# Turning the next block's input on VectorE instead of TensorE in an mLSTM + MLP kernel

## What is computed

```python
xn = layernorm(x)                       # per token, no scale or shift
q, k, v = xn @ Wq.T, xn @ Wk.T, xn @ Wv.T
i_pre, f_pre = soft_cap(xn @ Wig.T + big), soft_cap(xn @ Wfg.T + bfg)
h = mlstm_scan(q, k, v, i_pre, f_pre)   # 8 heads, a state that is carried from token to token
attn = (sigmoid(xn @ Wog.T) * multihead_norm(h, gamma)) @ Wout.T
ffn = (silu(xn @ w_gate.T) * (xn @ w_up.T)) @ w_down.T      # 2048 hidden features
return x + attn + ffn
```

## Time and profile before

| | |
|---|---|
| median of three runs | 3138.32 us |
| the profiled execution | 3138.3 us |
| its span, first to last instruction | 3136.5 us |
| TensorE busy | 3084.2 us, 98% |
| VectorE, ScalarE, GpSimd busy | 61%, 36%, 24% |
| before the first block's gates | 73.6 us |
| first block | 100.1 us |
| each of the 30 blocks between | 95.4 us |
| last block with the tail | 100.6 us |

### The profile page before, as it was taken

One profiled execution on the slowest core, in us unless ns is written; L12 is line 12 of the kernel. 1 busy time (PEld: TensorE's weight loads), 2 busy tenths in 40 slices (PEclk: granted clock), 3 DMA queues, 4 the chain that ended last, 5 costly groups with the idle time before them and its releaser, 6 DMA issues.

```text
span 3136.5 us, 61859 instructions
## 1 busy us (share of the span) xinstructions
PE 3084.2 (98%) x22474; PEld 2240.3 (71%) x22474; DVE 1907.1 (61%) x4377; ACT 1126.0 (36%) x2160; POOL 751.1 (24%) x1120
## 2 busy tenths in 40 slices
PE   4999999999999999999999999999999999999999
PEld 2677777777777777777777777777777777777776
DVE  8666656656556656555666566565566665565665
ACT  6333333333333333333333333333233333333332
POOL 4222222222222222222222222212222212222222
PEclk9999999999999999999999999999999999999999
DMA  5000000000000000000000000000000000000000
GB/s 222 8 14 13 13 7 7 13 13 13 13 6 8 13 13 13 7 7 13 13 13 13 7 7 13 13 13 13 0 13 13 13 13 7 7 13 13 13 13 7
DMA packets 20334, 51.09 MB, mean 16 GB/s; under 512 B 1506, under 2 KB 1634, under 8 KB 18274
## 3 DMA queue, kind: packets, MB, share of 16 engines
q1 hardware_dynamic: 20322, 50.95, 4.4%
HBM read 34.16 MB, written 16.78 MB: 16 GB/s over the span
## 4 chain that ended last, share of the span: by engine, by line
PE 97%; DVE 1%; ACT 1%; issue 0%; DMA 0%; SPq 0%; DVEq 0%; ACTq 0%
PE work L1082 21%; PE work L1084 21%; PE work L1083 21%; PE acc L1083 7%; PE acc L1084 7%; PE acc L1082 7%; PE o_bank L1195 3%; PE o_bank L1255 2%; PE work L1261 2%; PE s_bank L1242 1%; PE work L1273 1%; PE work L1267 1%; PE e_bank L1236 1%; PE work L1172 1%; PE work L1227 1%; DVE amax L740 1%
## 5 line engine op out<-in xcount | busy, mean ns | idle before, releaser
L1082 PE MATMUL work<-xt,weights 128*128 128x256 f16 x4608 | 1256.0, 273 | 0.5 <-DVE arena L958 0.5
L1084 PE MATMUL work<-xt,weights 128*128 128x256 f16 x4608 | 1256.0, 273 | 0.0
L1083 PE MATMUL work<-xt,weights 128*128 128x256 f16 x4608 | 1255.9, 273 | 0.0
L543 POOL TENSOR_TENSOR arena<-arena 128x256 f16<-128x256 f32 x512 | 348.4, 680 | 1715.7 <-ACT arena L678 1715.7
L955 DVE SCALAR_TENSOR_TENSOR arena<-arena,work 128x256 f32<-128x256 f32 x512 | 215.2, 420 | 538.1 <-ACT arena L674 534.9
L1082 PEld LDWEIGHTS work<-xt,weights 128*128 128x128 f16 x4608 | 478.5, 104 | 69.9 <-DVE arena L958 0.7
L1083 PEld LDWEIGHTS work<-xt,weights 128*128 128x128 f16 x4608 | 450.9, 98 | 69.5
L1084 PEld LDWEIGHTS work<-xt,weights 128*128 128x128 f16 x4608 | 450.8, 98 | 52.2
L674 ACT ACTIVATE arena<-work,unscale 128x256 f32<-128x256 f32 x512 | 241.7, 472 | 585.6 <-PE work L1084 585.2
L678 ACT ACTIVATE arena<-arena 128x256 f16<-128x256 f32 x512 | 213.3, 417 | 592.2 <-DVE arena L958 592.2
L1082 PE MATMUL acc<-weights,arena 128*128 128x512 f16 x1024 | 388.1, 379 | 0.4 <-POOL arena L543 0.4
(11 more groups left out here) (214 smaller groups left out, 4038.1 us busy)
## 6 DMA issues: line engine op xcount, KB each, us to landing
arena<-x_dram SPq DMA_DIRECT2D x33, 512.0 KB, 3.3
out_dram<-arena SPq DMA_DIRECT2D x32, 512.0 KB, 2.8
weights<-w_g_dram SPq DMA_DIRECT2D x4, 1024.0 KB, 12.6
weights<-w_u_dram SPq DMA_DIRECT2D x4, 1024.0 KB, 20.4
arena<-w_d_dram SPq DMA_DIRECT2D x4, 1024.0 KB, 26.8
arena<-w_qk_dram SPq DMA_DIRECT2D x1, 1024.0 KB, 5.8
arena<-w_v_dram SPq DMA_DIRECT2D x1, 1024.0 KB, 7.8
weights<-w_o_dram SPq DMA_DIRECT2D x1, 1024.0 KB, 25.3
```

Source lines behind the costliest of these rows:

```text
L543: g.tensor_tensor(hh[:, j % HB, 1, :], tt[:, j % 2, :], hh[:, j % HB, 0, :], ALU.subtract).then_inc(h_ready, 1)
L1082: t.matmul(dst, w[0], a[0], start=first, stop=False, skip_group_check=True)
L1083: t.matmul(dst, w[0], a[1], start=False, stop=False, skip_group_check=True)
L1084: return t.matmul(dst, w[1], a[0], start=False, stop=last, skip_group_check=True)
```

## The change

The next input's two chunks are no longer transposed by TensorE. VectorE turns each in sixteen pieces: one instruction takes 32 tokens and one 32-feature slice of each of the four 128-feature groups, turns the four 32x32 squares, and writes them to another group of 32 partitions (`turn`). Four calls of `turn` make a chunk. Three stand behind tile 5 and one behind tile 6 for chunk 0, three behind tile 7 and one behind tile 9 for chunk 1. For that the statistics' `mean_var` goes from tile 5 to tile 3, `xn0` from tile 6 to 4 and `xn1` from tile 9 to 6. `xn` and its turned form lie in SBUF space of the block that is free by then, so the high and low parts (`xT0`, `xT1` on ScalarE and VectorE, still behind tile 15) read SBUF and not PSUM. They wait for `hoT1` on TensorE, after which nothing in the block reads `xt`.

`USES` loses `xT0` and `xT1`; `att1` gets bank 1 by name. The gates wait for both low parts through `xt_ready`. On VectorE alone, behind tile 10, `pv2` comes before `es3`.

```diff
 USES = ([... "ffn12", "st3", "o1",
-         "ffn13", "att0", "ffn14", "ffn15", "hoT1", "xT0", "xT1", "att1"])
+         "ffn13", "att0", "ffn14", "ffn15", "hoT1", "att1"])
+BANK = {name: n % 3 for n, name in enumerate(USES)}
+BANK["att1"] = 1

-AFTER[3] = ["wT", "stack3"]
-AFTER[4] = ["wbc", "kT", "es0"]
-AFTER[5] = ["o0", "mean_var"]
-AFTER[6] = ["es1", "pv0", "xn0"]
+AFTER[3] = ["wT", "stack3", "mean_var"]
+AFTER[4] = ["wbc", "kT", "es0", "xn0"]
+AFTER[5] = ["o0", "turn00", "turn01", "turn02"]
+AFTER[6] = ["es1", "pv0", "turn03", "xn1"]
+AFTER[7] = ["turn10", "turn11", "turn12"]
 AFTER[8] = ["es2", "pv1", "center0"]
-AFTER[9] = ["scale0", "xn1"]
+AFTER[9] = ["scale0", "turn13"]
 AFTER[10] = ["heads0", "es3", "pv2"]
+DVE_AFTER[10] = ["heads0", "pv2", "es3"]

+            def turn(dst, src, q):
+                tokens = slice(q * 32, (q + 1) * 32)
+                for r in range(P // 32):
+                    features = src[tokens, :].rearrange("t (k r f) -> t r k f", k=KC, f=32)[:, r, :, :]
+                    d.transpose(dst.rearrange("p (k t) -> p k t", k=KC)[r * 32:(r + 1) * 32, :, tokens],
+                                features).then_inc(xn_turned, 1)

 (ScalarE)
                         elif step.startswith("xT"):
-                            wait_full(act, i, step)
-                            x_high(i + 1, k, bank(step)[:, :])
+                            wait_full(act, i, "hoT1")
+                            act.wait_ge(xn_turned, START + (i * NCH + k + 1) * TURNS)
+                            x_high(i + 1, k, xnt[k])

 (TensorE)
-                pe.wait_ge(work_free[bank_no("xT1")], START + i * uses_of(bank_no("xT1")))
+                pe.wait_ge(xt_ready, NCH * (i + 1))
...
-                        elif step.startswith("xT"):
-                            pe.wait_ge(xn_ready, NCH * (i + 1) + k + 1)
-                            for n in range(KC):
-                                tr = t.transpose(bank(step)[:, n * P:(n + 1) * P], xn[:, k, n * P:(n + 1) * P],
-                                                 ident[:, :])
-                            tr.then_inc(work_full, 1)
```

More of the change, by code:

```diff
@@ L56 @@
          "ffn6", "st0", "ffn7", "ffn8", "st1", "ffn9", "ffn10", "st2", "ffn11", "hoT0", "ffn12", "st3", "o1",
-         "ffn13", "att0", "ffn14", "ffn15", "hoT1", "xT0", "xT1", "att1"])
+         "ffn13", "att0", "ffn14", "ffn15", "hoT1", "att1"])
 NUSE = len(USES)
-assert NUSE % 3 == 0
+BANK = {name: n % 3 for n, name in enumerate(USES)}
+BANK["att1"] = 1
 def bank_no(name):
-    return USES.index(name) % 3
+    return BANK[name]
 def uses_of(b, before=NUSE):
-    return len(USES[b:before:3])
+    return len([name for name in USES[:before] if BANK[name] == b])
 AFTER = {j: [] for j in range(NJ)}
@@ L95 @@
 AFTER[15] = ["hoT1", "xT0", "xT1"]
+TURNS = 16
+DVE_AFTER = {j: list(steps) for j, steps in AFTER.items()}
+DVE_AFTER[10] = ["heads0", "pv2", "es3"]
 UNIT_IN = {j + 1: int(step[-1]) for j in AFTER for step in AFTER[j] if step.startswith("pv")}
@@ L229, in mlstm_mlp_kernel @@
                  ("hof", 512), ("hoh", 512), ("kp", 512), ("tt", 512), ("hh", 768), ("res", 1024),
-                 ("wtok", NCH * 72), ("xn", NCH * D), ("qq", 1024), ("kk", 1024),
+                 ("wtok", NCH * 72), ("qq", 1024), ("kk", 1024),
                  ("state", NG * GW), ("wr", 256), ("tg", 256), ("uhl", 256), ("xin", 1024)]
@@ L239, in mlstm_mlp_kernel @@
             at[name] = arena[:, starts[name]:starts[name] + n]
-        assert 5 * SLOT + GCOLS <= starts["xn"]
+        assert 5 * SLOT + GCOLS <= starts["qq"]
         def in_arena(n):
@@ L256, in mlstm_mlp_kernel @@
         xin = at["xin"].rearrange("p (c d) -> p c d", c=NCH)
-        xn = at["xn"].rearrange("p (c d) -> p c d", c=NCH)
+        xn_first = at["kk"].rearrange("p (c d) -> p c d", c=NCH)
+        xn = at["qs"], at["kf"]
+        xnt = at["kp"], arena[:, starts["lf"]:starts["lf"] + D]
         qs = at["qs"].rearrange("p (g t) -> p g t", g=NG)
@@ L331, in mlstm_mlp_kernel @@
         xt_hi = sem("xt_hi")
+        xn_turned = sem("xn_turned")
         xt_ready = sem("xt_ready")
@@ L514, in _ @@
             link(g.memset(uhl, 0.0))
+            pool.wait_ge(first_xt, NCH)
             for name in ("qq", "kk", "wr", "tg", "state"):
@@ L519, in _ @@
             for n, started in enumerate((*work_free, out_stored, res_done, exp_done, p_ready, num_ready, ho_ready,
-                                         state_ready)):
+                                         state_ready, xn_turned)):
                 g.memset(begun[0:1, n:n + 1], 0.0).then_inc(started, START)
@@ L604, in x_high, with norm_x @@
                              ACT.Copy).then_inc(xt_hi, 1)
-            def norm_x(i, c):
-                act.wait_ge(factors_ready, i + 1)
-                s.activation(xn[:, c, :], xin[:, c, :], ACT.Identity, bias=shift[:, c:c + 1],
+            def norm_x(dst, c):
+                s.activation(dst, xin[:, c, :], ACT.Identity, bias=shift[:, c:c + 1],
                              scale=rstd[:, c:c + 1]).then_inc(xn_ready, 1)
+            act.wait_ge(factors_ready, 1)
             for c in range(NCH):
-                norm_x(0, c)
+                norm_x(xn_first[:, c, :], c)
                 act.wait_ge(first_xt, c + 1)
@@ L710, in _ @@
                         elif step.startswith("xn"):
-                            norm_x(i + 1, k)
+                            if k == 0:
+                                act.wait_ge(factors_ready, i + 2)
+                                act.wait_ge(qi_ready, i + 1)
+                            else:
+                                wait_full(act, i, "kT")
+                            norm_x(xn[k], k)
                         elif step.startswith("xT"):
-                            wait_full(act, i, step)
-                            x_high(i + 1, k, bank(step)[:, :])
+                            wait_full(act, i, "hoT1")
+                            act.wait_ge(xn_turned, START + (i * NCH + k + 1) * TURNS)
+                            x_high(i + 1, k, xnt[k])
                 own.close()
@@ L800, in means, with x_low @@
                     d.bn_aggr(mean_var[:, c, :], bn6[:, c, :]).then_inc(stats_ready, 1)
-            def x_low(i, c, src, done):
+            def turn(dst, src, q):
[4 more added lines that the diff above has]
+                                features).then_inc(xn_turned, 1)
+            def x_low(i, c, src):
                 dve.wait_ge(xt_hi, NCH * i + c + 1)
                 d.tensor_tensor(xt[:, :, 1, c * P:(c + 1) * P], src.rearrange("p (k t) -> p k t", k=KC),
-                                xt[:, :, 0, c * P:(c + 1) * P], ALU.subtract).then_inc(done, 1)
+                                xt[:, :, 0, c * P:(c + 1) * P], ALU.subtract).then_inc(xt_ready, 1)
             back = 1.0 / (XS * WS)
@@ L825, in _ @@
             for c in range(NCH):
-                x_low(0, c, (e_bank, s_bank)[c][:, :], xt_ready)
+                x_low(0, c, (e_bank, s_bank)[c][:, :])
             scales(0)
@@ L960, in _ @@
                                            op1=ALU.mult).then_inc(free_of(f"ffn{j}"), 1)
-                    for step in AFTER[j]:
+                    for step in DVE_AFTER[j]:
                         k_ = int(step[-1]) if step[-1].isdigit() else 0
@@ L1061, in _ @@
                         elif step.startswith("xT"):
-                            wait_full(dve, i, step)
-                            x_low(i + 1, k_, bank(step)[:, :], free_of(step))
+                            x_low(i + 1, k_, xnt[k_])
+                        elif step.startswith("turn"):
+                            c = int(step[-2])
+                            dve.wait_ge(xn_ready, NCH * (i + 1) + c + 1)
+                            turn(xnt[c], xn[c], k_)
                         elif step == "att0":
@@ L1105, in _ @@
                 for k in range(KC):
-                    tr = t.transpose((e_bank, s_bank)[c][:, k * P:(k + 1) * P], xn[:, c, k * P:(k + 1) * P],
+                    tr = t.transpose((e_bank, s_bank)[c][:, k * P:(k + 1) * P], xn_first[:, c, k * P:(k + 1) * P],
                                      ident[:, :])
@@ L1141, in _ @@
             pe.wait_ge(w_split_act, len(PE_LOW))
-            pe.wait_ge(xt_ready, NCH)
             with pe.Fori(0, NB) as i:
```

## The result

| | time, us | block in the loop, us |
|---|---|---|
| kernel before | 3139.22, median of 4 runs (3137.84 to 3140.45) | 95.41 |
| changed kernel | 3115.12, median of 4 runs (3114.46 to 3116.27) | 94.68 |
| forecast | 3114.6 (3109 to 3128) | 94.67 |

The ratio is 0.9924 with a 95% interval from 0.9913 to 0.9936: 0.76% faster. The profiled execution has a span of 3112.7 us against 3136.5, 23.8 us less.

What follows compares the result with a forecast made beforehand. TensorE, busy 98% of the span, was taken to bound the kernel. 3138.3 - 28.2 (transposes) + 4.3 (bank of `att1`) + 0.2 (`mean_var`) = 3114.6 us, range 3109 to 3128 us; the turns cost nothing.

Steps and rivals of the forecast that it cites:

- The sum: Whole kernel: 3138.3 - 28.2 + 4.3 + 0.2 = 3114.6 us, 0.76% less.
- The transposes: TensorE before `down(14)`: eight float32 transposes gone, 0.88 us in each of 32 blocks, 28.2 us less.
- The bank of `att1`: Behind the gates: `q` waits for VectorE's drain of `att1`, 0.14 us, 31 times, 4.3 us.
- The turns' price: VectorE: 32 turns a block at 0.31 us each, 9.9 us a block; bounds 0.21 and 0.45 us a turn.
- Where they lie: VectorE, tiles 5 to 10: tile 7's L955 0.24 us late, tile 8's 0.9, last four turns end at 1570.9.
- `heads0`: VectorE behind tile 10: ends 1.3 us later, at 1574.5 and not 1573.18, still in time for `hoT0`.
- The spare time: `heads0` ends about 1.0 us before TensorE wants its result for `hoT0` at 1575.52.
- the first rival: Turns too slow: spare time gone at 0.36 us a turn, slower than before from 0.40; 3172 us at 0.45; chance 0.09.
- The exchange: VectorE behind tile 10, `pv2` before `es3`: L997 in front would take some 0.7 us of tile 12's spare 1.0.
- `mean_var`: Moved behind tile 3, it delays tile 4's L955 and L958 by 0.24 us; costs 0.24 us once, first block.
- `down(15)`: Comes 0.88 us earlier against GpSimd's low part: just fits; if not, some 0.1 us a block, 3 us in all.

Runs made afterwards that it cites:

- experiment 1: Changed kernel with `att1` in bank 2 in place of bank 1: 3110.76 us, ratio 0.9911 to the kernel before.
- experiment 6: Changed kernel with the turned squares written back to the 32 partitions they come from (output not the reference's): 3115.44 us.
- Experiment 4: Changed kernel with four more turns behind tile 7, into a buffer nothing reads: 3117.85 us; with eight more: 3159.61 us, ratio 1.0067.
- experiment 3: Changed kernel with eight transposes put back on TensorE behind `hoT1`, read by nobody: 3143.69 us, ratio 1.0016 to the kernel before.
- experiment 5: Changed kernel with `es3` before `pv2` on VectorE again: 3116.70 us; with four more turns behind tile 7 as well: 3159.76 us.

## Why the prediction was right, point by point

- **The sum.** Forecast 23.7 us less. The 32 blocks are 23.2 us shorter: 0.69 in the first, 0.73 in each of the 30 between, 0.71 in the last. The stretch ahead of the first block's gates is 0.6 us shorter (73.02 against 73.63) and makes it 23.8. The edit has no part in that: in the eight edits of the changed kernel this stretch takes from 73.4 to 75.6 us. That the total met the forecast within 0.5 us is in part luck; that the block did within 0.01 is not.
- **The transposes.** Forecast 28.2 us; put back, they cost 28.6. Right.
- **The bank of `att1`.** Forecast 0.14 us a block and 4.3 us; the trace shows 0.14 and experiment 1 gives back 4.4. Right, in place and size, and the 0.06 us from a release in the first block holds at q (1593.61 to 1593.67).
- **The turns' price.** I took 0.31 us from copies over 32 partitions and it is 0.33: 10.6 us a block and not 9.9. The form of the term (duration and hold) is what the trace shows. VectorE's busy time went up by 273.7 us and not 287: the turns are 309.4, but `heads0` has become shorter (below). The estimate of 0.34 from the Trainium skill ("VectorE: DVE Perf Modes", "The three transpose paths", with the hold) was the nearer one. The Trainium skill's rule on the same page, "Two Vector instructions with no wait between them", that an output in another quadrant (group of 32 partitions) than the last one's holds the instruction, agrees with experiment 6. The Trainium skill's advice there to give 128x128 transposes to TensorE ("Rules for kernel authors") does not hold here: 10.6 us on VectorE are free where 0.88 us on TensorE are not.
- **Where they lie.** Tile 7's L955 was to be 0.24 us late and is 0.35 (1544.23 + 11.33 against 1555.21); tile 8's 0.9 and is 1.2 (1549.02 + 11.33 against 1559.12); the last four turns were to end at 1570.9 and end at 1571.3. This follows from 0.33 in place of 0.31.
- **`heads0`.** Here a term was mis-sized, to the safe side. It was to end 1.3 us later than before and ends 0.9 later (1562.77 + 11.33 = 1574.10 against 1573.18), although the turns before it were slower. I moved its three instructions with the durations that they had. L1046 and the one behind it stood beside GpSimd's low part and mask and took 0.62 and 1.22 us; now L1070 is done before the low part begins (1561.42), L1073 overlaps it for its last 0.28 us, and they take 0.16 and 0.69. The last one takes 0.95 and not 0.69. Together 0.73 us less, against 0.34 us by which `heads0` begins later than forecast. That GpSimd's neighbourhood makes the difference is read from these coincidences; no run tests it. That the two errors of the prediction have opposite signs is luck.
- **The spare time.** Forecast 1.0 us, measured 1.42 to the end of the record. I charged no release there. Experiment 4 shows 0.15 us for it, which leaves 1.27. The threshold of 0.36 us a turn from the first rival is by this 0.33 + 1.27 / 20 = 0.39, worked out and not tried in this form.
- **The exchange.** The prediction had `es3` in front take 0.7 us of the spare time at tile 12. Without the exchange the drain of `st2` ends 1.5 us nearer to tile 12, as the scores also wait 0.75 us for GpSimd's mask, a wait that the prediction left out. All of the 1.51 us are used up, and the exchange is just needed.
- **`mean_var`.** Forecast 0.24 us once. In the first block q has no wait yet, and with the transposes put back (experiment 3) it is 0.20 us longer than before. In the changed kernel it is 99.43 us against 100.12, 0.69 less: 0.88 less 0.20 is 0.68. Right.
- **`down(15)`.** Forecast: it just fits. TensorE's weight load of `down(15)` now waits for GpSimd's low part, which ends at 1588.61. The load unit is idle for 0.22 us ahead of it, 0.10 more than ahead of its neighbours, and the matmul still starts at its time, 0.22 us behind the one before:

```profile
1588.66 0.10 PEld L1109 LDWEIGHTS acc<-weights,arena 128*128 128x128 f16 x1 [0.22 <-POOL arena L554]
```

```profile
1588.56 0.38 PE L1111 MATMUL acc<-weights,arena 128*128 128x512 f16 x1
1588.78 0.38 PE L1109 MATMUL acc<-weights,arena 128*128 128x512 f16 x1
```

  The load ends at 1588.76, 0.02 us ahead of its matmul: that is all the room there is, and the prediction had 0.03. What happens past it was not tried.

## What to carry to other kernels

Where one engine is dense, the gain of taking work from it is the work's pitch, less what the waits that move with it cost; a bank handed to another user is such a wait, and it was a sixth of the gain here, for one digit in a table. Work moved to an engine with idle time is free up to the spare time at the first point where the dense engine wants that engine's result, which can be read off the trace (1.3 us here) and has little to do with the total idle time (28 us). Put drains of shared banks ahead of work that may itself wait: the exchange is worth 0.05 us a block while there is room and 1.3 us once there is none.

## What the runs showed of the hardware

- A VectorE transpose of 32 partitions by 128 float32 elements takes 302 ns, and in a row they start each 0.33 us when each writes other partitions than the last; on the same partitions one takes 0.26 us and starts 0.19 us behind the last (experiment 6).
- GpSimd's work beside it did not slow it. This low part ran inside the first call of twelve turns of the changed kernel, which took 3.95 us:

```profile
1532.81 0.67 POOL L554 TENSOR_TENSOR arena<-arena 128x256 f16<-128x256 f32 x1 [2.86 <-ACT arena L688]
```

  It took its usual 0.67 us, and the turns took as long as elsewhere, as did the last four, beside its power (1558.72 to 1560.36). A float16 copy beside the same low part took 0.80 us and its neighbours 0.28.
- TensorE started 0.06 us after the end of the releasing record at a float16 matmul (q, and tile 12 in experiment 5), and 0.15 us after it at a float32 transpose (`hoT0` in experiment 4).
